# Strassen block products for the gate and up projections of the last feed-forward stage

## What is computed

```python
x = x + _L1_ffn_ref(_layernorm(x), w_gate_up, w_down)

def _L1_ffn_ref(x, w_gate_up, w_down):         # I = 1376 hidden features
    gate_up = einsum('bsh,oh->bso', x, w_gate_up)
    d = gate_up.shape[-1] // 2
    h = silu(gate_up[..., :d]) * gate_up[..., d:]
    return einsum('bsi,hi->bsh', h, w_down)
```

## Time and profile before

| | us |
|---|---|
| median of 3 runs | 1407.05 (1406.98 to 1407.35) |
| the profiled execution, its own time | 1404.97 |
| its span, from the first to the last instruction | 1403.1 |
| TensorE busy over the span | 1345.0 (96%) |
| VectorE / ScalarE / GpSimd busy | 1006.7 / 718.6 / 699.8 |

### The profile page before, as it was taken

One profiled execution on the slowest core, in us unless ns is written; L12 is line 12 of the kernel. 1 busy time (PEld: TensorE's weight loads), 2 busy tenths in 40 slices (PEclk: granted clock), 3 DMA queues, 4 the chain that ended last, 5 costly groups with the idle time before them and its releaser, 6 DMA issues. The chain is left out here.

```text
span 1403.1 us, 20386 instructions
## 1 busy us (share of the span) xinstructions
PE 1345.0 (96%) x6795; PEld 1076.5 (77%) x6795; DVE 1006.7 (72%) x2372; ACT 718.6 (51%) x1560; POOL 699.8 (50%) x619
## 2 busy tenths in 40 slices
PE   8999999987998999999999999999999999799999
PEld 5766666655676788888888888888888888688887
DVE  8888877775767878877787778777877788622322
ACT  3488886684544554544454545444545455433332
POOL 5589996683544554433542544335425442054453
PEclk9999999999999999999999999999999999999999
DMA  4000000100201011110110101101101010143332
GB/s 142 1 1 1 2 1 1 31 16 26 65 0 68 24 31 30 31 38 9 37 39 15 37 24 31 38 9 38 39 16 38 16 46 0 31 105 100 91 92 83
DMA packets 64950, 50.72 MB, mean 36 GB/s; under 512 B 5776, under 2 KB 54288, under 8 KB 64592
## 3 DMA queue, kind: packets, MB, share of 16 engines
q1 hardware_dynamic: 64848, 49.43, 12.2%
HBM read 47.32 MB, written 2.10 MB: 35 GB/s over the span
## 5 line engine op out<-in xcount | busy, mean ns | idle before, releaser
L1935 POOL TENSOR_TENSOR a_p_lo<-a_prob,a_p_hi 128x512 fp32r<-128x512 f32 x160 | 203.2, 1290 | 45.5 <-ACT a_p_hi L1789 44.0
L243 DVE CUSTOM_DVE_ANT_0 a_score<-a_score,mask_w 128x384 f32<-128x384 f32 (+3 forms) x384 | 195.9, 558 | 13.1 <-PE a_score L1386 11.4
L737 ACT ACTIVATE a_pt_hi<-a_ring 128x512 fp32r<-128x512 f32 x160 | 93.9, 596 | 164.3 <-PE a_ring L421 164.3
L890 POOL TENSOR_TENSOR a_rot_a<-a_rot_a,a_rot_b 128x512 f32<-128x512 f32 x79 | 102.3, 1296 | 147.5 <-DVE a_rot_b L599 147.5
L728 ACT ACTIVATE a_prob<-a_score,a_nmax 128x128 f32<-128x128 f32 (+3 forms) x256 | 132.0, 529 | 57.9 <-DVE a_nmax L243 57.8
L364 PE MATMUL a_xo<-h_hi,w_both 128*128 128x512 f32 x384 | 151.4, 394 | 2.7 <-PEq L1973 2.5
L366 PE MATMUL a_xo<-h_hi,w_both 128*128 128x512 f32 x384 | 150.9, 393 | 0.0
L365 PE MATMUL a_xo<-h_lo,w_both 128*128 128x512 f32 x384 | 150.2, 391 | 0.0
L2562 POOL TENSOR_TENSOR w_both<-raw,w_both 128x512 fp32r<-128x512 f32 (+2 forms) x63 | 87.1, 1407 | 116.0 <-ACT w_both L2506 115.9
L895 POOL TENSOR_TENSOR a_p_lo<-a_rot_a,a_p_hi 128x512 fp32r<-128x512 f32 x79 | 102.2, 1295 | 65.7 <-ACT a_p_hi L754 65.7
L579 DVE TENSOR_TENSOR a_pt_lo<-a_ring,a_pt_hi 128x512 fp32r<-128x512 f32 x160 | 108.5, 686 | 32.1 <-ACT a_pt_hi L737 31.2
(11 more groups left out here) (380 smaller groups left out, 3660.4 us busy)
## 6 DMA issues: line engine op xcount, KB each, us to landing
raw<-in_L_gate_up_t SPq DMA_DIRECT2D x40, 256.0 KB, 3.1
raw<-in_L_attn_wq SPq DMA_DIRECT2D x32, 256.0 KB, 2.8
raw<-in_L_attn_wo SPq DMA_DIRECT2D x32, 256.0 KB, 2.6
raw<-in_L_down_t SPq DMA_DIRECT2D x20, 256.0 KB, 2.6
raw<-in_L_attn_wk SPq DMA_DIRECT2D x8, 256.0 KB, 2.9
raw<-in_L_attn_wv SPq DMA_DIRECT2D x8, 256.0 KB, 2.9
out<-x SPq DMA_DIRECT2D x8, 256.0 KB, 2.2
x<-in_L_attn_x SPq DMA_DIRECT2D x3, 512.0 KB, 7.5
```

Of the source, the lines that this page charges most:

```text
L243: return nc.vector.tensor_tensor_reduce(scores, scores, m.mask_w[:, T - n:T], -1.0, LARGE, ALU.add, ALU.min, to)
L890: nc.gpsimd.tensor_tensor(of_a, of_a, of_b, ALU.add).then_inc(summed, 1)
L1935: nc.gpsimd.tensor_tensor(p_lo[:, mm % NP, :], prob[:, mm % NE, :], p_hi[:, mm % NP, :].bitcast(F32), ALU.subtract).then_inc(p_ready, 1)
```

## The change

**Gate and up.** From step 3 on (`PLAIN = 3`) the two logical products of a step are taken as one 2 x 2 block product and formed with seven half-size products in place of eight. The blocks on the weight side are the two halves of k (top and low, two k-tiles each) of the gate and of the up piece, those on the token side the same halves of k for the two halves of the tokens (256 columns each). Each of the seven (`product`) is 2 k-tiles x 3 = 6 matmuls of 256 columns. Their operands are sums and differences of blocks:

- of the weights, four combinations a step (`combine` on VectorE into `s_raw`; `combinations_high` on ScalarE; `combinations_low` on GpSimd, one instruction of 1024 elements). The up piece's own split is done for its lower half alone, so its w_hi and w_lo have 256 elements.
- of the input, once per batch: `whole` (h_hi + h_lo) and `difference` on VectorE into `mix`, then `t_hi` and `t_lo`. For the first batch this lies in the stage's head, for the second in the steps 3 to 10, in twelve instructions of 512 elements (`mix_second`), at most two a step.

Afterwards VectorE puts gate and up together out of the products' banks: four additions early in the step (`fold_early`; ScalarE first copies M1 out of its bank, `keep`) and three late (`fold_late`), 256 elements each, into `gate_sum` and `up_sum` in SBUF. Silu and `multiply` read those instead of banks.

**Down** of step s - 2 instead of s - 1 follows the products of step s (`LAG = 2`), and the down pieces move behind in the loading order. **The head**: TensorE does three `up` before the turns, and the weight splits and `mix` of the first batch are interleaved with the layer norm.

```diff
+    PLAIN = 3
...
+    LAG = 2
...
+    order = [(0, 0), (0, 1), (0, 2), (1, 0), (1, 1), (2, 0), (2, 1)]
+    order += [piece_of for s in range(PLAIN, ALL) for piece_of in ((s, 0), (s, 1), (s - 2, 2))]
+    order += [(ALL - 2, 2), (ALL - 1, 2)]
...
-        done = 0 if fresh else QT
-        ln = LayerNorm(nc, m, ctx, "n3", out, fresh=fresh, stats=True, first=done, count=NT - done)
+        bank12, bank67, bank4, bank53 = gbank[1], ubank[1], gbank[0], ubank[0]
+        ln = LayerNorm(nc, m, ctx, "n3", out, stats=True, first=QT, count=NT - QT, turns=out)
...
+            for s, p in order:
+                if s >= 2:
+                    sp.wait_ge(w_ready, place[s - 2, p])
+                    if p == 0 and fast(s - 2):
+                        sp.wait_ge(combined, COMBINED * (s - 2 - PLAIN + 1))
+                    load_feed_forward_piece(sp, m, inp, s, p)
...
+            def product(to, l_hi, l_lo, r_hi, r_lo):
+                for k in range(2):
+                    last = three(to, l_hi[:, k, :], l_lo[:, k, :], r_hi[:, k, :], r_lo[:, k, :], k == 0, k == 1)
+                last.then_inc(formed, 1)
...
+                pe.wait_ge(w_ready, place[s, 0])
+                if start:
+                    pe.wait_ge(silued, s - 1)
+                else:
+                    pe.wait_ge(folded, folded_at(s - 1, GATE_LEFT))
+                product(bank12[0:w, left], g_hi[:, top, :], g_lo[:, top, :], m.h_hi[:, top, first], m.h_lo[:, top, first])
+                product(bank12[0:w, half], g_hi[:, low, :], g_lo[:, low, :], m.h_hi[:, low, first], m.h_lo[:, low, first])
...
+                pe.wait_ge(s_ready, s - PLAIN + 1)
...
+                else:
+                    pe.wait_ge(folded, folded_at(s - 1, UP_SHARED))
+                product(bank67[0:w, left], combination(s_hi, s, S2), combination(s_lo, s, S2), t_hi[:, b, low, half],
+                        t_lo[:, b, low, half])
+                product(bank67[0:w, half], combination(s_hi, s, S3), combination(s_lo, s, S3), t_hi[:, b, top, half],
+                        t_lo[:, b, top, half])
...
+                product(bank4[0:w, left], u_hi[:, low, :], u_lo[:, low, :], t_hi[:, b, low, left], t_lo[:, b, low, left])
+                if start:
+                    pe.wait_ge(prodded, s)
+                else:
+                    pe.wait_ge(folded, folded_at(s - 1, UP_RIGHT))
+                product(bank53[0:w, left], combination(s_hi, s, S1), combination(s_lo, s, S1), t_hi[:, b, top, left],
+                        t_lo[:, b, top, left])
+                product(bank53[0:w, half], combination(s_hi, s, S4), combination(s_lo, s, S4), m.h_hi[:, low, second],
+                        m.h_lo[:, low, second])
+                for t in range(QT):
+                    down(s - LAG, t)
...
+            up(0, 0)
+            up(0, 1)
+            up(1, 0)
+            for t in range(ln.ring):
                 ln.turn(pe, t)
...
+            up(1, 1)
+            ln.turn(pe, ln.ring)
+            up(2, 0)
+            up(2, 1)
+            ln.wait(pe, QT)
+            for t in range(QT):
+                down(0, t)
+            for s in range(PLAIN, ALL):
+                products(s)
...
+                    wait_products(act, s - 2)
+                nc.scalar.activation(halves(s_hi, s), halves(s_raw, s), ACT.Copy).then_inc(s_hi_done, 1)
...
+                act.wait_ge(formed, formed_at(s, M2))
...
+                nc.scalar.activation(kept[0:w, s % 2, :], bank12[0:w, 0:N2], ACT.Copy).then_inc(kept_done, 1)
...
+                w = tiles[s % NM][1]
                 act.wait_ge(prodded, s + 1)
                 if s >= 2:
                     wait_down(act, s - 2)
                 nc.scalar.activation(z_hi[0:w, s % 2, :], prod[0:w, s % 2, :], ACT.Copy).then_inc(z_hi_done, 1)
...
+            for s in range(PLAIN, ALL):
+                hidden_high(s - 1)
+                keep(s)
+                if s + 1 < ALL:
+                    weights_high(s + 1, 0)
+                    combinations_high(s + 1)
+                    weights_high(s + 1, 1)
+                weights_high(s - 1, 2)
+                if s in (PLAIN + 3, PLAIN + 4):
+                    mix_high(1, s - PLAIN - 3)
+                gate(s)
+            hidden_high(ALL - 1)
+            weights_high(ALL - 1, 2)
...
+            def combine(s):
+
+                wait_loaded(dve, s, 0)
+                wait_loaded(dve, s, 1)
+                if s >= PLAIN + 2:
+                    dve.wait_ge(s_ready, s - 2 - PLAIN + 1)
+                g, u, n = piece(raw, s, 0), piece(raw, s, 1), COMBINED * (s - PLAIN)
+                c = [combination(s_raw, s, q) for q in range(COMBINED)]
+                nc.vector.tensor_tensor(c[S1], u[:, 0:2, :], u[:, 2:4, :], ALU.add).then_inc(combined, 1)
+                nc.vector.tensor_tensor(c[S3], g[:, 0:2, :], u[:, 0:2, :], ALU.subtract).then_inc(combined, 1)
+                dve.wait_ge(combined, n + 1)
+                nc.vector.tensor_tensor(c[S2], c[S1], g[:, 0:2, :], ALU.subtract).then_inc(combined, 1)
+                dve.wait_ge(combined, n + 3)
+                nc.vector.tensor_tensor(c[S4], g[:, 2:4, :], c[S2], ALU.subtract).then_inc(combined, 1)
...
+                nc.vector.tensor_tensor(mix[:, k, :], m.h_hi[:, k, tok].bitcast(F32), m.h_lo[:, k, tok].bitcast(F32),
+                                        ALU.add).then_inc(mixed, 1)
...
+                nc.vector.tensor_tensor(mix[:, to[0], to[1]], mix[:, x[0], x[1]], mix[:, y[0], y[1]],
+                                        ALU.subtract).then_inc(mixed, 1)
...
+            left, half = slice(0, N2), slice(N2, T)
...
+                dve.wait_ge(kept_done, s - PLAIN + 1)
+                if s >= PLAIN + 2:
+                    dve.wait_ge(silued, s - 1)
+                nc.vector.tensor_tensor(gate_sum[0:w, s % 2, left], kept[0:w, s % 2, :], bank12[0:w, half],
+                                        ALU.add).then_inc(folded, 1)
+                dve.wait_ge(formed, formed_at(s, M7))
+                nc.vector.tensor_tensor(common, kept[0:w, s % 2, :], bank67[0:w, left], ALU.add).then_inc(folded, 1)
+                dve.wait_ge(folded, folded_at(s, SHARED))
+                nc.vector.tensor_tensor(up_common, common, bank67[0:w, half], ALU.add).then_inc(folded, 1)
+                dve.wait_ge(formed, formed_at(s, M4))
+                dve.wait_ge(folded, folded_at(s, UP_SHARED))
+                nc.vector.tensor_tensor(up_sum[0:w, s % 2, left], up_common, bank4[0:w, left],
+                                        ALU.subtract).then_inc(folded, 1)
+
+            def fold_late(s):
+
+                w = tiles[s % NM][1]
+                dve.wait_ge(formed, formed_at(s, M3))
+                nc.vector.tensor_tensor(gate_shared[0:w, s % 2, :], shared[0:w, s % 2, :], bank53[0:w, left],
+                                        ALU.add).then_inc(folded, 1)
+                dve.wait_ge(folded, folded_at(s, GATE_SHARED))
+                nc.vector.tensor_tensor(gate_sum[0:w, s % 2, half], gate_shared[0:w, s % 2, :], bank53[0:w, half],
+                                        ALU.add).then_inc(folded, 1)
+                nc.vector.tensor_tensor(up_sum[0:w, s % 2, half], up_shared[0:w, s % 2, :], bank53[0:w, left],
+                                        ALU.add).then_inc(folded, 1)
...
-                dve.wait_ge(upped, s + 1)
                 if s >= 2:
                     dve.wait_ge(z_ready, s - 1)
...
+                up = up_sum[0:w, s % 2, :] if fast(s) else ubank[s % 2][0:w, :]
+                nc.vector.tensor_tensor(prod[0:w, s % 2, :], act_g[0:w, s % 2, :], up,
                                         ALU.mult).then_inc(prodded, 1)
...
                 dve.wait_ge(z_hi_done, s + 1)
                 nc.vector.tensor_tensor(z_lo[0:w, s % 2, :], prod[0:w, s % 2, :], z_hi[0:w, s % 2, :].bitcast(F32),
                                         ALU.subtract).then_inc(z_ready, 1)
...
+            for s in range(PLAIN, ALL):
+                hidden_low(s - 1)
+                if s < NM:
+                    mix_second(2 * (s - PLAIN))
+                fold_early(s)
+                if s + 2 < ALL:
+                    combine(s + 2)
+                fold_late(s)
+                multiply(s)
+                if s < NM:
+                    mix_second(2 * (s - PLAIN) + 1)
+                if s == NM + 1:
                     add_out(0)
+            hidden_low(ALL - 1)
             add_out(1)
...
+            def combinations_low(s):
+
+                pool.wait_ge(s_hi_done, s - PLAIN + 1)
+                nc.gpsimd.tensor_tensor(halves(s_lo, s), halves(s_raw, s), halves(s_hi, s).bitcast(F32),
+                                        ALU.subtract).then_inc(s_ready, 1)
...
+            for s in range(PLAIN - 1, ALL):
+                if s + 1 < ALL:
+                    weights_low(s + 1, 0)
+                    combinations_low(s + 1)
+                    weights_low(s + 1, 1)
+                weights_low(s - 1, 2)
```

(59 more changed lines are left out.)

210 lines of the change are left out of this document (156 added, 54 removed).

## The result

| | before | after |
|---|---|---|
| median, us | 1407.01 (4 runs, 1403.78 to 1407.35) | 1444.57 (4 runs, 1441.87 to 1445.03) |
| ratio | | 1.0267, 95% interval 1.0253 to 1.028 |
| profiled execution: its time, its span | 1404.97, 1403.1 | 1444.27, 1442.4 |

The kernel became slower by 37.6 us, 2.7%. I take the last stage by itself: its first matmul starts at 1214.32 before and at 1215.80 after, its last one ends at 1399.93 and 1439.20. So the stage went from 185.6 to 223.4 us, +37.8, and the 1.5 us left of the span's +39.3 lie ahead of it, where nothing is changed.

The account below looks back on a forecast made before the run. TensorE bounds the kernel before; after, VectorE's loop with waits for GpSimd does, 10.4 us a step against 8.16. Head +2, sixteen steps +35.8, mix +2.3, end -2.3: +37.8, a median of 1445 us, range 1412 to 1460.

Parts of the forecast that it names:

- The bound changes hands: Last stage: VectorE's loop replaces TensorE as the bound, TensorE standing some 2 us each step before M5.
- The timetable: One steady step, placed instruction by instruction from z_hi's end: 10.4 us, of which 3.7 are waits for GpSimd.
- The waits are for whole GpSimd instructions, in turns: VectorE instructions with two SBUF inputs each wait out one GpSimd instruction; six of thirteen a step exposed, where one was.
- TensorE's part: A step's 42 matmuls of 256 columns and 12 of 512 take 7.72 us, 0.44 less than 8.16.
- The sum: Whole last stage: head, steps and end together +37.8 us on a span of 1403.1.
- The head: Stage start until z_hi of step 3: about 2 us later than before, between -4 and +8.
- Steps 4 to 19: Sixteen steps at 10.4 in place of 8.16 us: +35.8, and +2.3 for the mix instructions.
- The end: From z_hi of step 19 to the last matmul: 15.7 us where 18.0 stood, -2.3.
- The phase: Order of the first combine and GpSimd's 1024 elements hardly matters: a step of 10.1 if combine comes first.
- VectorE keeping its turn: Rival: the four of combine run through after the 1024 elements; step 8.8 to 9.3, 1418 to 1427 us; 13%.
- The cover holding: Rival: TensorE stays the bound at 7.72 a step; 1399, or 1396 with the head's gap gone; 17%.
- the worse case: Rival: TensorE's clock falls to 1.2 GHz, +85 us, or combine loses to three GpSimd instructions; above 1460; 6%.

Follow-up runs that it names:

- e3_two_of_three: Changed kernel with hi x lo left out of each block product, 14 of 42 small matmuls a step; 1444.12 us, ratio 1.0265 to the kernel before.
- e1_memset_combinations: Changed kernel with GpSimd's 1024-element subtraction for the combinations replaced by a zero filling; 1403.23 us, ratio 0.9965 to the kernel before.
- e2_memset_all: Changed kernel with all GpSimd subtractions from step 3 on, combinations and weight pieces, replaced by zero fillings; 1399.48 us, ratio 0.9936 to the kernel before.
- e6_combine_last: Changed kernel with VectorE's combine(s + 2) moved behind the product of step s; 1420.66 us, ratio 1.0101 to the kernel before.
- e7_two_halves: Changed kernel with GpSimd's one 1024-element subtraction cut into two of 512; 1441.44 us, ratio 1.0249 to the kernel before.

## Why the prediction was right, step by step

- **The bound changes hands.** Shown: TensorE waits before M5 in 16 steps (forecast 2 us each; the row has 1.76, the mean is 1.5), and a third of the block products' matmuls less changes nothing (`e3_two_of_three`). The prediction had no wait for GpSimd's split ahead of M6; there are 11, 6.1 us in all. They lie in TensorE's spare time too.
- **The timetable.** With zero at the end of z_hi, 1339.13, the four of `combine` end at 4.80, 5.68, 7.11 and 7.56 (forecast 4.80, 5.68, 7.12, 7.56), the product at 9.80 (9.72) and z_hi at 10.46 (10.37). Most of the 0.09 is between Silu's end and the product's start. The prediction's terms for VectorE alone add up to 6.73, not 6.65, and `e1_memset_combinations` has 7.16 with one wait of 0.43, the same 6.73. The slip is in the limit of the rival below and not in the timetable.
- **The waits are for whole GpSimd instructions, in turns.** Shown by `e1_memset_combinations`, `e2_memset_all`, `e6_combine_last` and `e7_two_halves`. The rule of the Trainium skill (SBUF — State Buffer, Who interferes with whom), that two SBUF inputs contend with a GpSimd instruction that reads SBUF and not with one that only writes it, agrees with them: 0.42 beside the filling and 2.51 beside the subtraction. The turns themselves the prediction read from one place, and from another kind of instruction (L140 in the earlier trace rows is a TENSOR_SCALAR, with one full-size input); that additions with two inputs take turns in the same way is first shown by the changed kernel and `e7_two_halves`.
- **TensorE's part.** The step without other limits is 7.78, not 7.72 as the rows gave, and 0.6 above the 7.18 of the estimate by the formula that the Trainium skill gives for a single matmul by itself (TensorE: Matmul & The Clock Gate, Back-to-back issue gap).
- **The sum.** The head: z_hi of step 3 ends 40.8 us into the stage, 36.9 before: +3.9 where +2 stood, within its bounds of -4 to +8. Steps 4 to 19: 166.5 against 130.8, +35.7, where +38.1 stood with `mix`. The steady 10.46 would give 36.8; the mix steps 4 to 6 were 10.78, 1.0 in all rather than 2.3; and the 96-wide tile of the first batch, which I had left at full price, made two steps 9.82 and 8.94, 2.2 less; `add_out` and the last of the sixteen make most of the rest. The end: 16.1 against 17.9, -1.8 (forecast -2.3; the last matmul before ends at 1399.93, where the prediction has 1399.8). In all +37.8: the head was sized too low by 1.9, the steps too high by 2.4, the gain at the end too high by 0.5, and they cancel. The steady step is a hit of the mechanism; that the median, 1444.57, lies 0.4 from the forecast is luck.
- **The phase.** The prediction held that it hardly matters (10.1 if the first of `combine` comes in before the 1024 elements). In the step of 8.94 three of them came in before (0.41 each) and only the fourth waited, 2.47. That one step is 1.5 shorter than a steady one; the next was back at 10.47. No run tried to hold the kernel in that phase.
- **The rivals.** VectorE keeping its turn: against it stand all the steady steps. The cover holding: it would have needed waits under 1.0 us a step (1.1 in the prediction); they are 3.7. Its 1399 or 1396 is where `e2_memset_all` came out, 1399.5 beside a before of 1408.0. The cause of the worse case, a fall of the clock, did occur in small (below), without a cost.

## What to carry to other kernels

Before VectorE and GpSimd get the work of a smaller matrix product, count the VectorE instructions that take both inputs from SBUF beside GpSimd's. Here each cost up to the whole GpSimd instruction that it met, and what followed it in program order paid. Put them where GpSimd is idle or where nothing waits behind them (38 us of loss fell to 14 by the place of one call), and let GpSimd's long instructions run under VectorE's work out of banks. Here the saving of 0.38 us a step paid only where VectorE and GpSimd had two steps' time for its additions. The additions alone would have fitted into one (6.7 of 7.78 us); whether an order exists that keeps the waits out of it, no run shows.

## What the runs showed of the hardware

- The clock. TensorE's granted clock was 0.91 from 1260 to 1280 us and 0.93 from 1340 to 1360 in the changed kernel, so a part of each stretch was at 1.2 GHz, though TensorE was busy for over 80% of them and its longest idle time from 1250 to 1440 was 1.8 us. From 1339.27 to 1341.83 its matmuls of 512 columns follow each other after 0.43 us in place of 0.23. The wait ahead of the next M5, at 1347.87, is 0.85 in place of 1.76, and the step is 10.46 all the same, as it is about 10.5 from 1300 to 1320, where the clock was 1.00: what was lost lay in TensorE's spare time. In `e3_two_of_three` the mean was 0.96 over 1300 to 1390, at 70% busy. A kernel that leaves such gaps and is bound by TensorE again afterwards could pay for them; no run here shows that.
- A filling by GpSimd of 1024 elements takes 0.96 us, against 2.38 for the subtraction, and did not hold up the VectorE instruction that ran inside it. In `e2_memset_all`, with fillings alone from step 3 on, z_lo takes 0.69 in every step (682 to 695 ns over 22).
- The last stage started at 1214.3 to 1219.3 us in the profiled executions of eleven kernels (before, after and the nine runs) that have the same work ahead of it. That is more than what some of them change, so the stage by itself tells small changes better than the span. What moves it was not looked into.
